# Self-attention: value matmuls two steps behind their scores instead of three

## What is computed

```python
def attention(x, ctx, wq, wk, wv, wo, bo):         # 16 heads of 64
    q, k, v = x @ wq, ctx @ wk, ctx @ wv           # split into heads
    sim  = einsum('bhid,bhjd->bhij', q, k) * 64 ** -0.5
    attn = softmax(sim, axis=-1)
    out  = einsum('bhij,bhjd->bhid', attn, v)
    return out @ wo + bo

x = x + attention(layer_norm(x), layer_norm(x), ...)   # self, 1024 keys
x = x + attention(layer_norm(x), context, ...)         # cross, 77 keys
x = x + geglu_ff(layer_norm(x), ...)
```

## Time and profile before

| | us |
|---|---|
| median of 3 runs (lowest to highest) | 2636.36 (2632.66 to 2638.06) |
| the profiled execution's own time | 2637.65 |
| its span, first to last instruction | 2635.9 |
| PE busy | 2260.3 (86%) |
| DVE busy | 1762.0 (67%) |
| ACT busy | 1587.1 (60%) |
| POOL busy | 1236.2 (47%) |

### The profile page before, as it was taken

One profiled execution on the slowest core, in us unless ns is written; L12 is line 12 of the kernel. 1 busy time (PEld: TensorE's weight loads), 2 busy tenths in 40 slices (PEclk: granted clock), 3 DMA queues, 4 the chain that ended last, 5 costly groups with the idle time before them and its releaser, 6 DMA issues.

```text
span 2635.9 us, 58536 instructions
## 1 busy us (share of the span) xinstructions
PE 2260.3 (86%) x24644; PEld 1434.2 (54%) x24644; DVE 1762.0 (67%) x3202; ACT 1587.1 (60%) x2124; POOL 1236.2 (47%) x756
## 2 busy tenths in 40 slices
PE   5999987779799998777969999878797999987878
PEld 2666655455366665545526666554553666654455
DVE  5888874644688887464358888746446888874743
ACT  2878773633388887373238888736334888872732
POOL 2665662640265656264026565626502656562640
PEclk7999998889699999898969999989897999997979
DMA  2212110210222221020022222102002121200200
GB/s 65 72 51 67 51 43 10 58 33 1 49 60 58 60 58 36 19 63 19 2 79 61 57 60 58 36 15 64 22 1 59 49 69 48 68 25 21 65 15 17
DMA packets 64021, 116.26 MB, mean 44 GB/s; under 512 B 16758, under 2 KB 21008, under 8 KB 63760
## 3 DMA queue, kind: packets, MB, share of 16 engines
q1 hardware_dynamic: 63760, 112.52, 16.4%
HBM read 50.77 MB, written 2.10 MB: 20 GB/s over the span
## 4 chain that ended last, share of the span: by engine, by line
PE 58%; DVE 18%; issue 7%; ACT 6%; POOL 5%; DMA 4%; POOLq 2%; SPq 1%; DVEq 0%; ACTq 0%
PE work L768 7%; PE scores L688 7%; PE scores L690 7%; PE scores L689 7%; PE scores L810 6%; DVE minima L1128 6%; PE scores L799 6%; DVE prob L1151 4%; PE work L830 3%; PE work L834 3%; PE work L688 3%; PE work L690 3%; PE work L832 3%; PE work L689 3%; POOL prob L655 2%
## 5 line engine op out<-in xcount | busy, mean ns | idle before, releaser
L655 POOL TENSOR_TENSOR prob<-prob 128x1024 f16<-128x1024 f32 (+1 forms) x320 | 685.5, 2144 | 709.6 <-ACT prob L995 701.6
L994 ACT ACTIVATE prob<-scores 128x1024 f32<-128x1024 f32 (+1 forms) x576 | 592.4, 1028 | 251.0 <-PE scores L810 228.8
L1128 DVE TENSOR_REDUCE minima<-work 128x1 f32<-128x512 f32 x1024 | 684.6, 684 | 76.8 <-PE work L768 61.8
L995 ACT ACTIVATE prob<-scores 128x1024 f16<-128x1024 f32 (+1 forms) x576 | 588.8, 1022 | 0.0
L830 PE MATMUL work<-vals,prob 128*128 128x65 f16 (+1 forms) x4608 | 496.3, 195 | 59.0 <-POOL prob L655 50.6
L830 PEld LDWEIGHTS work<-vals,prob 128*128 128x128 f16 (+1 forms) x4608 | 437.8, 100 | 130.8 <-POOL prob L655 63.8
L832 PE MATMUL work<-vals,prob 128*128 128x64 f16 (+1 forms) x4608 | 496.4, 195 | 0.0
L834 PE MATMUL work<-vals,prob 128*128 128x65 f16 (+1 forms) x4608 | 496.4, 197 | 0.0
L832 PEld LDWEIGHTS work<-vals,prob 128*128 128x128 f16 (+1 forms) x4608 | 435.4, 98 | 58.2 <-issue 1.4
L834 PEld LDWEIGHTS work<-vals,prob 128*128 128x128 f16 (+1 forms) x4608 | 435.9, 99 | 0.0
L768 PE MATMUL work<-ka,qa 128*128 128x512 f16 x1024 | 402.8, 397 | 34.1 <-DVE minima L1128 19.6
(11 more groups left out here) (127 smaller groups left out, 4014.0 us busy)
## 6 DMA issues: line engine op xcount, KB each, us to landing
raw_odd<-in_pieces SPq DMA_DIRECT2D x40, 512.0 KB, 3.7
raw_even<-in_pairs SPq DMA_DIRECT2D x53, 384.0 KB, 3.2
qa<-staged_q SPq DMA_DIRECT2D x128, 128.0 KB, 2.3
ka<-staged_k SPq DMA_DIRECT2D x128, 128.0 KB, 2.3
qb<-staged_q SPq DMA_DIRECT2D x64, 128.0 KB, 2.3
kb<-staged_k SPq DMA_DIRECT2D x64, 128.0 KB, 2.4
qa<-qa SPq DMA_DIRECT2D x64, 128.0 KB, 2.3
raw_odd<-in_pairs SPq DMA_DIRECT2D x13, 384.0 KB, 3.2
```

The lines of the kernel that those rows point to most:

```text
L655: pool.tensor_tensor(prob[1][0:kr, slot, :], prob32[0:kr, slot, :], prob[0][0:kr, slot, :], ALU.subtract).then_inc(a.polished, 1)
L994: act.activation(prob32[0:kr, n % shape.ring, :], source, ACT.Exp)
L995: act.activation(prob[0][0:kr, n % shape.ring, :], source, ACT.Exp)\
L1128: dve.tensor_reduce(minima[:, t, h:h + 1], out[:, :], AX.X, ALU.max, negate=True)\
```

## The change

One constant becomes 2 instead of 3:

```diff
-RING, LAG = 4, 3
+RING, LAG = 4, 2
```

## The result

| | before | after |
|---|---|---|
| median, us | 2636.86 | 2716.11 |
| lowest to highest, us | 2632.66 to 2638.06 | 2710.42 to 2717.33 |
| runs | 4 | 4 |
| span of the profiled execution, us | 2635.9 | 2713.2 |

The ratio is 1.0299, with a 95% interval of 1.028 to 1.0318. The kernel became 3% slower; 2712.8 us had been forecast.

The account below looks back on a forecast made before the run. PE nearly sets the pace in self-attention, so new waits lengthen it unless covered by old ones. Per round 0.72 + 7 x 2.17 + 3.2 = 19.1 us, four rounds 76.4 us: 2712.8 us, range 2680 to 2738 us.

Parts of the forecast that it names:

- First unit, 0.55 us: Steps 5 to 7: the gather of value 3, now ahead of `combine`, lengthens DVE's unbroken row: +0.55 us.
- Second unit, 1.07 + 0.55 = 1.62 us: Value 1 waits for polish 1 behind POOL's split, +1.07 us; later the gather stands ahead of `combine`, +0.55 us.
- two waits overlap and the larger counts: Second unit: PE's waits for the gather behind refine 0 and for polish 1 overlap; 1.07 us counts, not their sum.
- one of the signs: PE's wait at the shift (L781 for L1137) should be about as long or longer though value 4 arrives later.
- POOL first: Second unit: refine 0 starts after L600 and stands until it ends; some 1.8 us more a unit, 2763 us; 4%.
- Gathers find room: DVE is not last at the shifts; only POOL chain, first and last pair cost: 46 us, 2682 us; 6%.
- Not slower: All new waits fall into PE's idle 1.87 us a pair; at most 6.4 us gained, 2630 us; 5%.
- The clock: Each pair loses 5 us to half clock; 30 pairs add 75 us, 2788 us; 2%.
- First pair, 0.72 + 0.55 us: Stage's first unit: step 2 gets value 0, one more block, +0.72 us; gather ahead of `combine`, +0.55 us.
- Last pair, 3.2 us: PE gets stuck for polish 3 one step earlier, so score 6 and value 4 come after: 3.2 us, bounds 2.0 and 4.0.
- The sum: A round: 0.72 + 7 x 2.17 + 3.2 = 19.1 us; four rounds: 76.4 us.

Follow-up runs that it names:

- pool4: Low part of step 4 also moved to GpSimd, in the kernel before (lag 3) and the changed kernel (lag 2): 2623.53 and 2664.24 us.
- short gather: Self-attention gather cut to one copy of 8 columns, no reciprocal or scaling, at lag 3 and in the changed kernel (lag 2): 2635.85 and 2687.08 us.
- pool4_lag2: Changed kernel (lag 2) with the low part of step 4 on GpSimd too: 2664.24 us, ratio to before 1.0105.
- three short kernels: Changed kernel (lag 2) with the gather cut short, the piece split cut short, or both: 2687.08, 2701.97 and 2659.78 us.
- gather_first_lag2: Changed kernel (lag 2) with the gather put ahead of the low part in a step's order: 2744.90 us, ratio to before 1.0402.
- late_split_lag3: Kernel before (lag 3) with the piece split of every second unit moved from step 2 to step 7: 2634.68 us, ratio 0.999.

## Why the prediction was right

**First unit, 0.55 us.** Measured 0.53 (21.13 to 21.66 us). It comes from DVE's row: the gather can be seen in it, with pool4 the term goes to zero, with the short gather to 0.08. That value 4 waits 0.6 us was right too (0.53), and so was that this wait is not the cost: PE's old wait at the shift covered it.

**Second unit, 1.07 + 0.55 = 1.62 us.** Measured 1.62 (22.83 to 24.45 us). pool4_lag2 shows the first part by itself (1.08). That two waits overlap and the larger counts is shown by the three short kernels together. The gather's wait was 1.12 us where 1.2 had been worked out, and that for the polish 0.31 us where 0.3 had. The wait at the shift, over the whole span, grew from 44.0 to 47.6 us, as one of the signs had it.

**The rivals.** *POOL first* is a real mechanism, as gather_first_lag2 shows, and stayed 0.67 us away from deciding in the pattern pair. The 4% rest on that one pair; in pairs 1, 3 and 5 only 0.13 to 0.64 us were left. An L600 that starts first takes 2.12 us, where 1.98 had been worked out. *Gathers find room* is false as long as refine 4 is on DVE, and true in pool4_lag2. *Not slower* is false: PE's idle places did take part of the waits, but what made the stage longer was DVE's and POOL's row and not PE's waits. *The clock* stood at 1.00 in the second unit with its waits of 1.12 and 1.09 us; it didn't fall.

**First pair, 0.72 + 0.55 us: right, but covered by something else.** From the first score of the stage to that of the second unit, the changed kernel takes 0.2 us less in the first stage and 2.3 to 2.6 us more in the other three, instead of 1.27. The first scores of the single steps tell the parts from each other. From step 2 to step 3, across the added value block, the delay grows by 0.72 to 0.73 us in all four stages, and from step 6 to step 7 by 0.54 to 0.55 us: both terms are there at their size. The rest has come about before step 2 (1.4 us less in the first stage; 1.4, 1.4 and 1.0 us more in the others), and there the granted clock differs. First score at 59.24 us before and 59.46 us after in the first stage, at 711.24 and 726.99 us in the second; stretches of 3 us around and behind these moments, the kernel before and then the changed one:

```profile
59.00:62.00 3.00, 2.76 (x7) 1.04 (x8) 0.59 (x2) 0.84 (x1) 1.78 (x3) 0.50 0.00 0
...
714.00:717.00 3.00, 2.88 (x13) 1.12 (x12) 1.72 (x4) 2.30 (x4) 1.50 (x1) 0.95 0.00 0
```

```profile
59.00:62.00 3.00, 2.54 (x12) 1.18 (x13) 1.65 (x3) 1.47 (x2) 1.77 (x3) 1.00 0.00 0
...
730.00:733.00 3.00, 3.00 (x9) 1.08 (x8) 0.67 (x3) 1.45 (x2) 1.24 (x1) 0.50 0.00 0
```

In the first stage the changed kernel already has the full clock (1.00, 2.4 GHz) where the one before has half (0.50, 1.2 GHz); in the second, 3 us behind the first score, it still has half where the one before has 0.95. The change doesn't touch what comes ahead of the stages, and the moment isn't tied to the lag. In gather_first_lag2 the first units of the four stages take 20.71, 20.70, 23.47 and 20.70 us, with a clock of 1.00, 1.00, 0.50 and 1.00 in their first 3 us; at lag 3, late_split_lag3 has 1.00 there in one stage and 0.50 in three. What sets the moment no run here shows, and I had no term for it.

**Last pair, 3.2 us: mis-sized.** Its two units became longer by 1.7, 1.4, 2.2 and 4.1 us in the four stages, on the mean 2.4, where 2.0 and 4.0 us had been the bounds. PE's wait was 4.88 us and not 5 to 6. (In the fourth stage PE's wait before was only 2.08 us and not 4.18, so there was less to begin with and more to lose.) The step that failed is "nearer to the upper end, since PE and not ACT is late": I had put score 7 at half clock as before, but with score 6 and value 4 ahead of it score 7 now comes 5.3 us after PE has resumed and not 1.6, and the clock is up by then (its first matmul 0.39 instead of 0.61 us). So I read ACT's additional pair of exponentials (2.04 us) as most of the loss; no run separates it. The scatter goes with the clock: after the wait PE worked at 0.50 for 6.3, 6.0, 5.4 and 3.4 us before and for 4.7, 3.3, 3.3 and 5.9 us in the changed kernel, so that three stages got time back and the fourth, with the largest loss, did not.

**The sum.** The four stages are longer by 15.8, 18.3, 18.3 and 21.5 us, 73.9 us together; 76.4 had been forecast. By place, over the four stages: 12.2 us in the first units of pairs 1 to 6 (13.2 forecast), 45.1 us in the second units of pairs 0 to 6 (45.4), 7.2 us in the first units of the stages (5.1) and 9.5 us in the last pairs (12.8). What lies between them adds 3.4 us, which nothing in the change explains and which I had at zero. The span grew by 77.3 us. The closeness of the total, 2716.1 against 2712.8, owes something to luck: the last pair was forecast too long, and the clock at the start of the stages and the time between them, for which there was no term, made up for it; the 2.17 us a pair, which carries four fifths of it, owes nothing to them.

## What to carry to other kernels

A software pipeline's lag is not only the latency of its own chain: whatever is tied to the delayed step moves with it, here the gather, which empties a PSUM bank, slid from behind the critical instruction of VectorE's row to ahead of it. So ask of every queue what new thing now stands in front of its most urgent instruction, and take as its price the length of what is inserted, not the wait that shows on TensorE. And where two waits overlap, removing one shows little: 14 and 29 us alone, 56 together.

## What the runs showed of the hardware

The refine on VectorE and the split on GpSimd do not share, they take turns: in gather_first_lag2 a shift of about half a microsecond turned a refine of 1.22 us into one of 2.26 to 3.15 us, in 10 of 20 units of one execution, so that equal units of one kernel lasted from 24.7 to 27.8 us. From the end of an instruction on GpSimd to the start of the value matmul that waits for it there are 0.05 to 0.06 us (274.85 to 274.91 us in the changed kernel); behind the gather or `combine` on VectorE there are 0.15 us (259.46 to 259.61 us, 260.86 to 261.01 us). Waits of 1.12 and 1.09 us left the granted clock at 1.00, waits of 4.18 and 4.88 us were followed by 0.50, and so was a wait of 2.08 us in the fourth stage of the kernel before, ahead of which PE had been busy for only part of the time (1.88 of 3.9 us up to 2348.9 us; 0.50 from 2349.3 to 2352.7 us). After the wait of 4.88 us the clock was back at full speed when score 7 started, 5.3 us after PE had resumed (397.60 to 402.88 us).
